# Sorting the point cloud's features with the one-hot matrices as moving operand, both batches in TensorE's column halves

## What is computed

```python
def graph_features(feats, inds_list, perm, W, b):   # feats (2, 1024, 64)
    center = feats[:, :, None, :]
    for inds in inds_list:                  # 4 sort orders of the points
        neigh = gather(feats, inds)         # windows of 10 in sorted order
        gf = concatenate([broadcast(center), neigh - center], axis=-1)
    allf = stack(per_method, axis=-1)[..., perm]
    x = allf.reshape(B * N, 10, 512).astype(float16)
    qh = x.reshape(B * N, 10, 8, 64)
    attn = softmax(einsum("bihd,bjhd->bhij", qh, qh) / 8)
    out = einsum("bhij,bjhd->bihd", attn, qh).reshape(B * N, 10, 512)
    return (out @ W.T + b).reshape(B, N, 10, 128)
```

## Time and profile before

| | us |
|---|---|
| median of 3 runs | 1067.68 |
| the profiled execution, its own time | 1066.81 |
| its span | 1065.2 |
| TensorE (PE) busy | 1003.7 |
| VectorE (DVE) busy | 754.2 |
| ScalarE (ACT) busy | 455.9 |
| GpSimd (POOL) busy | 438.7 |

### The profile page before, as it was taken

The page is one execution under the profiler, slowest core; times in us unless marked ns, Lnnn a source line. Parts: engine busy times, 40 slices in busy tenths (PEclk is TensorE's granted clock), DMA queues, the critical chain, the costliest instruction groups (busy, mean ns, idle before and its releaser), DMA issues. The chain is left out here.

```text
span 1065.2 us, 38584 instructions
## 1 busy us (share of the span) xinstructions
PE 1003.7 (94%) x16232; PEld 768.2 (72%) x16232; DVE 754.2 (71%) x1898; ACT 455.9 (43%) x701; POOL 438.7 (41%) x408
## 2 busy tenths in 40 slices
PE   4899789999999999999989999989889999998998
PEld 2799777796968879557876777769876666664585
DVE  7598893756648375975678999967578888996310
ACT  6243233241432314212247777752356676662010
POOL 1101263030220202200169999950378888886000
PEclk9999889999999999999999999999999999999999
DMA  8997666878778783864313222224122222221550
GB/s 333 406 387 267 223 248 255 328 285 293 298 244 346 265 325 124 311 240 114 53 27 73 69 67 67 69 62 77 30 50 60 58 57 58 57 61 30 229 246 21
DMA packets 58363, 181.40 MB, mean 170 GB/s; under 512 B 10041, under 2 KB 10793, under 8 KB 57898
## 3 DMA queue, kind: packets, MB, share of 16 engines
q1 hardware_dynamic: 55850, 171.80, 47.3%
q0 software_dynamic: 2432, 8.42, 2.2%
HBM read 150.26 MB, written 0.56 MB: 142 GB/s over the span
## 5 line engine op out<-in xcount | busy, mean ns | idle before, releaser
L535 PEld LDWEIGHTS ps<-hT,ring 128*128 128x128 f32 x2304 | 262.3, 194 | 13.3 <-ACT xc L666 6.8
L535 PE MATMUL ps<-hT,ring 128*128 128x128 f32 x2304 | 264.2, 278 | 6.6 <-ACT xc L666 6.6
L1806 POOL TENSOR_TENSOR X<-sortedT,ring 128x960 f16 (+1 forms) x84 | 156.9, 1867 | 0.0
L937 POOL TENSOR_TENSOR y_y<-y_z,sgate 128x512 f32<-128x512 f32 x16 | 20.0, 1270 | 217.0 <-DVE y_z L872 200.8
L1824 POOL TENSOR_TENSOR S<-S,den 128x480 f32<-128x480 f32 x86 | 86.6, 1007 | 37.9 <-DVE den L1743 37.9
L1831 POOL TENSOR_TENSOR PP<-S,PP 128x480 f16<-128x480 f32 x86 | 97.9, 1138 | 3.5 <-ACT PP L1615 3.5
L571 PE MATMUL ps<-wt,y_n 128*128 128x512 f32 x224 | 99.1, 595 | 0.0
L782 DVE SCALAR_TENSOR_TENSOR xc<-xpad,parg,xc 128x128 f32<-128x128 f32 x192 | 58.3, 366 | 56.4 <-ACT xc L666 55.2
L1519 PE MATMUL ps<-PT,ring 128*64 128x120 f16 x2752 | 96.1, 221 | 2.0 <-DMA PT<-P_turned 1.7
L1615 ACT CAST PP<-S 128x480 f16<-128x480 f32 x86 | 66.9, 778 | 60.9 <-POOL S L1824 54.6
L1519 PEld LDWEIGHTS ps<-PT,ring 128*64 128x64 f16 x2752 | 81.8, 110 | 14.8 <-DMA PT<-P_turned 6.1
(11 more groups left out here) (322 smaller groups left out, 1607.2 us busy)
## 6 DMA issues: line engine op xcount, KB each, us to landing
ring<-in_w_in SPq DMA_DIRECT2D x36, 2048.0 KB, 8.7
wt<-in_w_out SPq DMA_DIRECT2D x14, 2048.0 KB, 7.8
PT<-P_turned SPq DMA_DIRECT2D x344, 64.0 KB
ring<-in_w SPq DMA_DIRECT2D x8, 1024.0 KB, 12.0
ctx_chunks<-in_ctx SPq DMA_DIRECT2D x4, 1024.0 KB, 8.9
ring<-in_ctx SPq DMA_DIRECT2D x4, 1024.0 KB, 16.6
krow<-keys_scratch POOLq DMA_DIRECT2D x8, 512.0 KB, 6.4
mchunk<-in_mask_t POOLq DMA_DIRECT2D x8, 512.0 KB, 8.6
```

The lines of the kernel that those rows point to most:

```text
L535: mm = nc.tensor.matmul(ps[:, bank, j * T:(j + 1) * T], weights[:, j, kc * P:(kc + 1) * P], k.hT[:, kc, :], start=kc == 0, stop=kc == KC - 1)
L1806: ins = gp.tensor_tensor(fcopy(c.X[u][:, 0, 0:1], full(cnt)), fcopy(c.fsT[:, 0, bass.ds(it * STEP, 1)], trio(start, cnt, 1)), fcopy(c.fTr[ ...
```

## The change

The operands of the sort's matmuls change places. The features' part (128 points x 64 channels of one batch) is now stationary, the one-hot is moving, 512 places at a time, and the result comes out with (batch, channel) on the partitions and places along the free axis: batch 0 in PSUM partitions 0 to 63, batch 1 in 64 to 127, in the same bank. An item is one chunk of one method with both batches. `sort_order` now runs over the batches innermost, and a class `SortPlan` lists the items, the builds, the evictions and their order. The transposes back (L1464) and their copies (L1593) are gone.

ScalarE evicts a method in four pieces of 32 partitions into a new buffer `gathered`, one strip of 32 partitions per method (128 partitions x 4 x 1024 fp32). DMAs copy a strip to its rows in `fsT`, two per strip, issued by SP and once by ScalarE. The last method is computed in two parts, a head of 256 places and a rest of 768, with the third method between them. The third method's eviction is split in the same places. The order is method 0, 1, head of 3, 2, rest of 3; in layer 2, where method 0 takes the buffers left over, it is rest of 0, head of 0, 1, head of 3, 2, rest of 3. Heads have buffers of their own. GpSimd's first differences wait for the heads, its eighth step for the rests. The transposes of X in step 0 wait for the last eviction but one, the first weighted rows for the last one.

The unsorted rows are first written to DRAM (`rows_kept`), and read back in 8 DMAs that repeat each row group four times; they now stand first in SP's queue, ahead of the zeros and the weights. The statistics move to a free slot of `ring`.

```diff
-PERMS = 10
+PERMS, HEAD = 10, 256
...
-    return j // (NM * NT), j // NT % NM, j % NT
+    return j % B, j // (B * NT), j // B % NT
...
+PER_METHOD = B * NT
+SPANS = {"full": (0, N), "head": (0, HEAD), "rest": (HEAD, N)}
+class SortPlan:
+    def __init__(self, layer):
+        opening = [(0, "full")] if layer == 1 else [(0, "rest"), (0, "head")]
+        phases = opening + [(1, "full"), (3, "head"), (2, "full"), (3, "rest")]
+        self.items = [(kind, i * PER_METHOD + B * t) for i, kind in phases for t in range(NT)]
+        self.consumed = {(kind, j + x): at + 1 for at, (kind, j) in enumerate(self.items) for x in range(B)}
+        here = lambda kind, j: j < PERMS and kind != "head"
+        self.builds = [(kind, j + x) for kind, j in self.items for x in range(B) if not here(kind, j + x)]
+        self.built = {build: at + 1 for at, build in enumerate(self.builds)}
+        self.evictions = [(i, kind, span) for i, kind in phases for span in ((SPANS["head"], SPANS["rest"]) if i == 2 else (SPANS[kind],))]
+        self.phase_end = {(i, kind): NT * (at + 1) for at, (i, kind) in enumerate(phases)}
+    def freed(self, kind, j):
+        if kind == "head":
+            return self.consumed.get((kind, j - (NM - 1) * PER_METHOD), 0)
+        return self.consumed["rest" if ("rest", j - PERMS) in self.consumed else "full", j - PERMS]
+PLAN = {1: SortPlan(1), 2: SortPlan(2)}
+SORT_BANKS, HEAD_BANKS = (2, 0, 2, 4), (4, None, None, 7)
+def sorted_pieces(i, kind):
+    if kind == "head":
+        return [(0, HEAD, HEAD_BANKS[i])]
+    begin = SPANS[kind][0]
+    return [(begin, begin + HALF, SORT_BANKS[i]), (begin + HALF, N, SORT_BANKS[i] + 1)]
...
+        self.gathered = sb("gathered", [P, 2 * B, N])
+        self.heads = slots(7, 2).bitcast(F16).rearrange("p (j n) -> p j n", n=HEAD)
...
+        self.stats = slots(10, 1)[:, 0:B * STEPS * 6].rearrange("p (b s w) -> p b s w", b=B, w=6)
...
+        def place_sorted(eng, i, r, span):
+            cols, to = slice(*span), r * C + methods[i] * CH
+            at = (2 * i + r) * CH
+            return eng.dma_start(c.fsT[to:to + CH, :, cols], c.gathered[at:at + CH, :, cols])
...
+            sp.dma_start(c.rows_kept, src[:, :]).then_inc(c.kept, 16)
+            sp.wait_ge(c.kept, 16 * layer)
+            for a in range(2):
+                for b in range(B):
+                    for r in range(2):
+                        at = b * C + (a * 2 + r) * CH
+                        sp.dma_start(c.fTr[r * C:(r + 1) * C, a * B + b, :],
+                                     bass.AP(tensor=c.rows_kept.tensor, offset=c.rows_kept.offset + at * N,
+                                             ap=[[0, NM], [N, CH], [1, N]])).then_inc(s_cc, 16)
...
-            for a in range(2):
-                for b in range(B):
-                    for r in range(2):
-                        for m in range(NM):
-                            at, to = b * C + (a * 2 + r) * CH, r * C + m * CH
-                            sp.dma_start(c.fTr[to:to + CH, a * B + b, :], src[at:at + CH, :]).then_inc(s_cc, 16)
...
+            for made, (i, kind, span) in enumerate(plan.evictions):
+                sp.wait_ge(s_row, row0 + made + 1)
+                if i < 2 and (kind == "full" or kind == "head"):
+                    for r in range(2):
+                        place_sorted(sp, i, r, SPANS["full"]).then_inc(c.landed[i], 16)
+                elif i >= 2 and span == SPANS["head"]:
+                    for r in range(2 if i == 3 else 1):
+                        place_sorted(sp, i, r, span).then_inc(c.head_in, 16)
+                elif i >= 2:
+                    for r in range(2):
+                        place_sorted(sp, i, r, span).then_inc(c.rest_in, 16)
...
-            for i, (b, m) in enumerate(order):
-                if i >= 2:
-                    pe.wait_ge(s_row, row0 + i - 1)
-                for at in range(NT):
-                    j = i * NT + at
-                    t = sort_order(layer, j)[2]
-                    if i == 0 and at in (0, NT // 2):
-                        pe.wait_ge(s_wc, wc0 + (1 if at == 0 else 2))
-                    if j >= PERMS:
-                        pe.wait_ge(s_perm, perm0 + j - PERMS + 1)
-                    for pt in range(NT):
-                        for s in range(2):
-                            mm = nc.tensor.matmul(ps[:, (i + halves[0]) % 2, pt * C:(pt + 1) * C], c.perm[:, perm_buffer(layer, j), pt * P:(pt + 1) * P],
-                                                  c.spl[:, s, t, b * C:(b + 1) * C], start=at + pt + s == 0,
-                                                  stop=at == NT - 1 and pt == NT - 1 and s == 1)
-                    mm.then_inc(s_ord, 1)
-                if i % NM == NM - 1:
-                    pe.wait_ge(s_row, row0 + i + 1)
-                    for n_turned, (half, a) in enumerate(turned_order):
-                        g = i // NM * 4 + n_turned
-                        if g >= 2:
-                            pe.wait_ge(s_sc, sc0 + g - 1)
-                        for j in range(4):
-                            mm = nc.tensor.transpose(ps[:, 2 + g % 2, j * P:(j + 1) * P], c.fsg[:, 4 * half + j, a * P:(a + 1) * P], k.ident[:, :])
-                        mm.then_inc(s_st, 1)
+            waited = 0
+            for at, (kind, j) in enumerate(plan.items):
+                i, t = j // PER_METHOD, sort_order(layer, j)[2]
+                if at in (0, NT // 2):
+                    pe.wait_ge(s_wc, wc0 + (1 if at == 0 else 2))
+                first, last = at % NT == 0, at % NT == NT - 1
+                if first and (i, kind) == (2, "full"):
+                    pe.wait_ge(s_row, row0 + (1 if layer == 1 else 2))
+                made = plan.built.get((kind, j + B - 1), 0)
+                if made > waited:
+                    pe.wait_ge(s_perm, perm0 + made)
+                    waited = made
+                for lo, hi, bank in sorted_pieces(i, kind):
+                    for part in range(2):
+                        for x in range(B):
+                            b = sort_order(layer, j + x)[0]
+                            perm = (c.heads[:, (j + x) % PER_METHOD, lo:hi] if kind == "head" else c.perm[:, perm_buffer(layer, j + x), lo:hi])
+                            mm = nc.tensor.matmul(ps[b * C:(b + 1) * C, bank, 0:hi - lo], c.spl[:, part, t, b * C:(b + 1) * C], perm,
+                                                  start=first and part == 0, stop=last and part == 1)
+                mm.then_inc(s_ord, 1)
...
-                    pe.wait_ge(s_sc, sc0 + 8)
+                    pe.wait_ge(s_row, row0 + len(plan.evictions) - 1)
...
+                if not after(it, 1):
+                    pe.wait_ge(s_row, row0 + len(plan.evictions))
...
-            for i, (b, m) in enumerate(order):
-                act.wait_ge(s_ord, ord0 + NT * (i + 1))
-                if i == NM:
-                    act.wait_ge(s_st, st0 + 4)
-                sc.mul(fcopy(c.fsg[:, :, m * CH:], [[2 * P, NT], [C, NHEAD], [1, CH]]),
-                       ps[:, (i + halves[0]) % 2, :].rearrange("p (t h c) -> p t h c", t=NT, h=NHEAD), 1 / SCALE).then_inc(s_row, 1)
-                if i % NM == NM - 1:
-                    for n_turned, (half, a) in enumerate(turned_order):
-                        g = i // NM * 4 + n_turned
-                        act.wait_ge(s_st, st0 + g + 1)
-                        sc.copy(c.fsT[:, a * B + b, half * HALF:(half + 1) * HALF], ps[:, 2 + g % 2, :]).then_inc(s_sc, 1)
+            for made, (i, kind, (begin, end)) in enumerate(plan.evictions):
+                act.wait_ge(s_ord, ord0 + plan.phase_end[i, kind])
+                if layer == 2 and made == 0:
+                    act.wait_ge(c.head_in, 64)
+                    act.wait_ge(c.rest_in, 64)
+                    for x in c.landed:
+                        act.wait_ge(x, 32)
+                bank, lag = sorted_pieces(i, kind)[0][2], 0 if kind == "full" else begin
+                for b in range(B):
+                    for a in range(2):
+                        rows = slice((b * 2 + a) * 2 * CH, (b * 2 + a + 1) * 2 * CH)
+                        ins = sc.mul(c.gathered[2 * i * CH:2 * (i + 1) * CH, a * B + b, begin:end],
+                                     ps[rows, bank:bank + (2 if end - lag > HALF else 1), :].rearrange("p a n -> p (a n)")[:, begin - lag:end - lag], 1 / SCALE)
+                ins.then_inc(s_row, 1)
+                if (i, begin) == (2, 0):
+                    act.wait_ge(s_row, row0 + made + 1)
+                    place_sorted(act, i, 1, SPANS["head"]).then_inc(c.head_in, 16)
...
-            for j in range(PERMS, PRODUCTS):
-                v.wait_ge(s_ord, ord0 + j - PERMS + 1)
-                at = rank_column(layer, j)
-                vec.tensor_scalar(c.perm[:, perm_buffer(layer, j), :], c.iota[:, :], k.rank[:, at:at + 1], None, ALU.is_equal).then_inc(s_perm, 1)
-                if j == 3 * NT:
+            waited = 0
```

(41 more changed lines are left out.)

18 lines of the change are left out of this document (6 added, 12 removed).

## The result

The changed kernel takes 1085.6 us (median; 1082.8 to 1087.9), the kernel before 1068.4; the ratio is 1.016, with a 95% interval of 1.0137 to 1.0182. It is slower by 17 us, where 7.5 us faster was forecast, and outside the range given. The profiled execution took 1082.8 us, its span is 1081.2, against 1065.2.

A forecast was written before the change was run, and what follows sets the result against it. TensorE was busy 94%; time from first sort matmul to first exponential comes off one for one. Gains 7.0 and 2.9 make 9.9, less 2.4 for the port is 7.5: 1059.3, with 0.87 to the median 1060.2 us; range 1054.5 to 1070.

The forecast's parts named there:

- TensorE's share: Sort products on TensorE: column halves overlap fully, 28.1 us per layer (27.3 to 29.2).
- The walk: Both engines stepped through the sort's phases: products end at 29.4 and 31.8 us, first exponentials at 33.7 and 36.1.
- Rivals 3 and 4: Sort: weight loads exposed, about 1070 us, chance 0.05; halves don't overlap for fp16 at full clock, 1107, chance 0.03.
- VectorE's share: One-hot builds: 0.40, 0.33, 0.20 us for full, rest, head, fixed part 0.13; sums 26.3 and 29.2 us.
- Rivals 1 and 2: VectorE bounds the sort throughout, about 1066 us, chance 0.16; slower still, builds taking full duration, 1075, chance 0.09.
- ScalarE and the tail: After the last product: last eviction ends 3.0 us later, then table load 1.28, then the first exponential.
- The moved DMAs: SP's queue: eight fourfold reads 6.5 us issue, 2.5 to land; all done near 20 us, needed at 28; cost nothing.
- the port: SBUF port shared by GpSimd and VectorE: first differences hold the builds 0 to 3 us per layer; 1.2 taken, 2.4 in all.
- The DMA latency of the heads: Third method's head strips to the differences: 2.5 us to land (4.1 at worst), costing nothing up to 3.8.
- One port hit of 1.9 us a layer in half the cases: Port alternative by the Trainium skill's rule: a GpSimd difference costs up to 1.9 us; gain would be 7.1.
- Rival 2: Builds take 0.48, 0.28, 0.41 us; sort walk ends at 37.2 and 41.2, time 1075 us; chance 0.09.
- Rival 3: Weight loads exposed before each matmul pair, 8.6 to 9.6 us; sort ends 35.9 and 37.7, about 1070 us; chance 0.05.

The follow-up runs named there:

- e3: Changed kernel with centre reads as 16 DMAs of 16 rows x 2, and zeros and conv weights ahead of the round trip; 1066.6 us, ratio 0.9986; profiled twice.
- e11: e9 with half of the centre reads left out (rows of methods 2 and 3 not copied); 1057.1 us, ratio 0.9904 to the kernel before.
- e6: e3 plus a row of unused matmuls before the first scores, layer weights behind the last build, exponential table loaded ahead of the evictions; 1065.9 us, ratio 0.9977.
- e7: e6 with layer 1's zeros written by GpSimd memsets instead of two DMAs; 1074.5 us, ratio 1.0061 to the kernel before.
- e9: e8 with VectorE's layer weights moved ahead of the last 16 builds, the rests; 1062.9 us, ratio 0.995 to the kernel before.
- e8: e3 with conv weight DMAs behind the centre reads, exponential table ahead of the evictions, and a short row of unused matmuls behind the products; 1064.4 us, ratio 0.9955.
- e10: Changed kernel with each fourfold centre read split into two twofold reads (outermost dimension 2, 16 DMAs of 128 KB); 1116.2 us, one run.
- e1: Changed kernel with the eight fourfold centre reads as 16 reads of 16 rows x 2 (outermost dimension 16), same bytes and queue place; 1069.5 us, ratio 1.0013.

## Why the prediction was wrong

**TensorE's share: right.** The walk had the products end at 29.4 and 31.8 us; they end at 29.2 and 32.3. Halves overlap fully: in the window 496 to 500 above, 40 records of 512 columns lie in 4.00 us, two per 0.2 us. Rivals 3 and 4 did not come true.

**VectorE's share: right.** The groups of builds, by form:

```profile
L1741 DVE TENSOR_SCALAR ring<-iota,rank 128x1024 f16<-128x1024 f16 x70 | 28.6, 480 | 1.8 <-PE ps L1519 1.8
...
L1741 DVE TENSOR_SCALAR ring<-iota,rank 128x768 f16<-128x768 f16 x38 | 12.8, 414 | 1.5 <-PE ps L1519 1.5
...
L1741 DVE TENSOR_SCALAR ring<-iota,rank 128x256 f16<-128x256 f16 x48 | 9.7, 279 | 0.0
```

One lasts 0.48, 0.41 and 0.28, and takes 28.6 / 70 = 0.41, 12.8 / 38 = 0.34 and 9.7 / 48 = 0.20 of the engine: the fixed part of 0.13 with overlapping starts holds down to 256 columns. Rivals 1 and 2 did not come true. TensorE's weight loads waited for it 1.2 us in layer 1 and 3.3 in layer 2.

**ScalarE and the tail: nearly right in size, but not the bound.** The eviction of the last rest and the table load ended at 527.93 in layer 1, 34.2 us behind the start against 33.7 in the walk (5.0 us behind the last product, not 4.3). In layer 1 that was 20.7 us too early to matter.

**The moved DMAs: the step that failed.** It had the eight reads at 6.5 us of issue and 2.5 to land, all of SP's early work done near 20 us after the sort's start, and "cost nothing". The reads took 29 us to the last landing, the zeros 16 and 33 us to land instead of 6.8, and the last head strip landed 50.4 us after the start, where the walk needed it at 28.1. The price came from the earlier trace rows, which are of DMAs with 16 and 128 partitions outermost; the new shape, with a broadcast of 4 outermost, had no row, and I bounded the cost by issue time alone, not by bytes over a rate. The sentence that X would be late if the DMAs were was there, without a number for how late they could be. Against the walk the first exponentials came 21.2 us late in layer 1 and 3.6 in layer 2. The shape of the reads is 2.5 of layer 2's (e3 has 37.2 there); the other 1.1 are 0.5 of products and 0.6 of the tail. In layer 1, e3 gives back 16 to 20 us of the 21.2; the rest is load on the DMA engines, which the sum didn't have either. The 1.5 us behind the exponentials have no cause that the runs show. The 2.4 us for the port were not spent (no build over 0.49 us), and the small terms give -0.3: 21.2 + 3.6 + 1.5 - 2.4 - 0.3 = 23.6, the distance from -7.5 to +16.0.

Mending the shape and the order alone didn't bring the forecast's gain: by its ratio e3 is 1.5 us under the kernel before (the interval is from 3.1 under to 0.2 over). The step was wrong twice, in the rate of the reads and in leaving the bytes ahead of the strips out of the sum.

**The DMA latency of the heads: right on a quiet queue, wrong in layer 1.** 2.5 us was the latency of 64 KB copies on a quiet queue, and 2.7 us with the issue is what the walk had. In e3 the differences began 3.1 us behind the end of the last head's eviction in layer 2, near the walk and within its bound of 3.8, but 5.1 in layer 1 and 8.8 in its second run, with the DMA share at 1.0. That is a question of load: in e11 it is 3.1 in layer 1 too.

**The port: not decided in the sort, shown elsewhere.** X came behind the last build in the kernel after. In e6 two operations of VectorE were stretched by 1.6 us each beside the differences, close to the 1.5 that I had allowed for one. In e7 a memset, which is longer, cost 5.9 us. In e9 and e11 layer 2's X did come over 2 us before the last product (28.2 against 30.8), beside the last builds, and there GpSimd was the side that was held: its first two differences took 5.2 us in both, against 3.70 in the kernel after:

```profile
754.70 5.22 POOL L1872 TENSOR_TENSOR X<-sortedT,ring 128x960 f16<-128x960 f32 x2 [48.08 <-DMA sortedT<-gathered]
```

That is e9's. The 1.5 us are of the predicted size, but they fell on GpSimd; the builds kept their 0.41 us.

**The side sums.** Three don't come out of their own terms. One port hit of 1.9 us a layer in half the cases makes 1.9 us over both layers, and a gain of 8.0, not 7.1. Rival 2's walk ends some 2 us too late: its builds, with the layer's weights, sum to 31.9 and 36.0 us, and the main walk ends 3.1 and 2.6 us behind such sums, not 5. Rival 3's layer 1 is 0.8 too low at 35.9, as 28.1 + 8.6 is already 36.7. None of them enters the forecast.

**Was the rest of the walk worth its 7.5 us?** Not shown for the kernel as it was predicted. e11 comes to the first exponentials in 33.1 and 34.3 us, together 12.3 us less than the kernel before, and its time is 1% less (ratio 0.9904, 7.7 to 12.7 us of 1068.4). But it leaves out copies, and has the table load ahead and the weights moved, which the walk didn't. With all of the copies, e9 keeps 5.3 us (3.2 to 7.5).

What stays open: why the same kernel's copies into 16 partitions run at 173 GB/s in one execution and at 142 in another, and how much of e9's layer 1 a layout of the centres over more partitions would give back. Neither that layout nor a read of four copies with the 16 rows outermost was tried, nor the write of the rows ahead of the zeros, which in e8, e9 and e11 held the reads back until 499.5 to 500.8 us.

## What to carry to other kernels

Price a DMA by its shape and its bytes over a rate read from a DMA of that shape, not by its issue time and another one's latency; a short outermost dimension is the first thing to look at. When DMAs are moved on a queue, write down for each one behind them when it is issued, when it lands and when it is needed. When work moves from an engine to DMAs, the DMA engines' busy share, not the latency, decides when the last small transfer lands.

## What the runs showed of the hardware that I had not expected

- A read with an outermost dimension of 4 or 2 kept 4 or 2 of the 16 DMA engines busy (share 0.25 and 0.13, 80 to 107 and 53 GB/s, in the kernel after and in e10).
- A queue with slow DMAs at its head holds the issuing engine too: SP's issue of two DMAs of zeros took 10.2 us instead of 1.4, and one small DMA 7.2.
- Copies into 16 partitions at a time held all 16 DMA engines busy at 120 to 196 GB/s (windows of 4 us in e1, e3, e8 and e9), where copies into 128 partitions ran at 360 to 389 (e3, e8, e11).
- The 512 KB write of the rows, issued behind 2 MB of zeros, was in flight for 8.8 us (e8) against 2.8 on a free queue, and held everything that waited for it.
- A memset of GpSimd of 7 us stopped two `tensor_scalar` operations of VectorE on SBUF for all of its length.
- After 23 us of idle time at the granted clock 0.50, layer 1's loop lost nothing that can be seen (192.2 us from its first exponential to layer 2's sort, 192.4 before; 191.1 to 193.6 over all kernels). GpSimd is the busy engine in that loop.
